# A GNN layer and a pair-routed expert layer on one core: GELU's table load, the first aggregation and the last group's ranks moved

## What is computed

```python
# x: (32, 256, 128), adj: (32, 256, 256)
def _L0_gnn_ref(x, adjacency, epsilon, W1, b1, rms_weight, W2, b2):
    neighbor_sum = jnp.einsum('bnm,bmd->bnd', adjacency, x)
    agg = epsilon * x + neighbor_sum
    h = jnp.einsum('bnd,dh->bnh', agg, W1) + b1            # H = 512
    h = jax.nn.silu(_rmsnorm(h, rms_weight))
    out = jnp.einsum('bnh,hd->bnd', h, W2) + b2
    return out
...
    logits = jnp.einsum('bsd,de->bse', xn, Wr) + br        # E = 8 experts
    top_vals, top_idx = jax.lax.top_k(logits, K)           # K = 2
    w = jax.nn.softmax(top_vals, axis=-1)
...
        h = jax.nn.gelu(jnp.einsum('bsd,dh->bsh', xn, W1[e]) + b1[e], approximate=False)
        y_e = jnp.einsum('bsh,hd->bsd', h, W2[e]) + b2[e]  # H = 256
        y = y + y_e * w_full[..., e, None]
...
    x = x + _L0_gnn_ref(_layernorm(x, axis=-1), adj, ...)
    x = x + _L0_ffn_ref(_layernorm(x, axis=-1), ...)
```

## Time and profile before

| | us |
|---|---|
| median of 3 runs | 423.39 |
| lowest and highest run | 420.89 and 424.64 |
| the profiled execution's own time | 420.72 |
| its span, first to last instruction | 418.9 |

### The profile page before, as it was taken

How to read it: one execution, slowest core, us unless ns; L and a number is a source line. 1 busy time by engine, 2 the same in 40 slices (tenths; PEclk the granted TensorE clock), 3 DMA queues, 4 the chain that set the end, 5 groups by cost and what they waited for, 6 DMA issues and landing times. The chain is left out here.

```text
span 418.9 us, 11379 instructions
## 1 busy us (share of the span) xinstructions
PE 382.8 (91%) x2598; PEld 322.7 (77%) x2598; DVE 301.4 (72%) x1290; ACT 280.2 (67%) x652; POOL 314.2 (75%) x440
## 2 busy tenths in 40 slices
PE   0899999999999999999879899998878999999994
PEld 0457676767777667766659899987768999999994
DVE  5677689898999999988874563665546666756562
ACT  1377677887777887778868556776657787454541
POOL 1223378877787888888888788999857767999984
PEclk9999999999999999999999999999999999999998
DMA  7879974444334442121164324555545543343311
GB/s 236 255 240 323 319 221 138 139 142 139 117 85 132 154 139 79 64 78 53 53 156 126 105 93 137 146 145 154 149 130 140 151 113 104 112 113 106 102 40 38
DMA packets 43473, 57.26 MB, mean 137 GB/s; under 512 B 6224, under 2 KB 36176, under 8 KB 42768
## 3 DMA queue, kind: packets, MB, share of 16 engines
q1 hardware_dynamic: 35200, 36.74, 31.6%
q0 software_dynamic: 6096, 18.52, 12.6%
q10 hardware_dynamic: 2112, 1.27, 1.1%
HBM read 41.80 MB, written 22.31 MB: 153 GB/s over the span
## 5 line engine op out<-in xcount | busy, mean ns | idle before, releaser
L569 POOL DMA_INDIRECT out<-result,rows_in x92 | 90.2, 980 | 29.5 <-DVE result L1553 17.6
L810 PE MATMUL banks<-w_sb,hidden_e 128*128 (+1 forms) x736 | 100.9, 279 | 0.1
L810 PEld LDWEIGHTS banks<-w_sb,hidden_e 128*128 128x128 f32 x736 | 91.0, 192 | 0.7 <-issue 0.3
L950 ACT ACTIVATE hidden_e<-banks 128x512 f32<-128x512 f32 x92 | 55.0, 597 | 44.7 <-PE banks L793 42.9
L512 POOL DMA_INDIRECT rows_dram<-rows_out,row_of x64 | 65.3, 1021 | 14.5 <-issue 10.4
L639 PE MATMUL banks<-gw_sb,agg 128*128 128x512 f32 x128 | 65.2, 595 | 0.9 <-DVE gw_sb L997 0.9
L525 POOL MEMSET space<- 128x620 f32 x100 | 62.9, 629 | 0.1
L661 PE MATMUL banks<-hidden_t,gw_sb 128*128 128x256 f32 x256 | 61.5, 383 | 1.5 <-ACT hidden_t L873 1.5
L661 PEld LDWEIGHTS banks<-hidden_t,gw_sb 128*128 128x128 f32 x256 | 46.5, 190 | 15.3 <-ACT hidden_t L873 7.3
L1090 DVE TENSOR_TENSOR hidden<-banks,rms_bc 128x512 f32<-128x512 f32 x64 | 43.9, 687 | 19.5 <-ACT hidden L858 19.4
L943 ACT ACTIVATE xg_t<-banks,ones 128x128 f32<-128x128 f32 x92 | 33.4, 363 | 24.6 <-PE banks L773 24.5
(11 more groups left out here) (147 smaller groups left out, 738.7 us busy)
## 6 DMA issues: line engine op xcount, KB each, us to landing
rows_in<-rows_dram SPq DMA_DIRECT2D x92, 132.5 KB, 2.2
adj<-adj_t SPq DMA_DIRECT2D x16, 512.0 KB, 4.9
x_tok<-x SPq DMA_DIRECT2D x16, 256.0 KB, 5.3
x_d<-x_t SPq DMA_DIRECT2D x16, 256.0 KB, 4.9
rows_dram<-idle_in POOLq DMA_DIRECT2D x1, 3710.0 KB, 13.8
rows_dram<-idle_in SPq DMA_DIRECT2D x28, 132.5 KB
out<-result,rows_in POOLq DMA_INDIRECT x92, 2.7
w_sb<-w SPq DMA_DIRECT2D x1, 1024.0 KB, 8.2
```

The costliest lines, as they stand in the source:

```text
L569: nc.gpsimd.indirect_dma_start(out=out, out_offset=bass.IndirectOffsetOnAxis(ap=rows_in[:, i % RING][:, IDX_AT:IDX_AT + 1].bitcast(U32), a ...
L810: last = pe.matmul(y_ps(i)[:, w], hidden_e[:, i % 4, w * HCE + c], w2_sb[:, bass.ds(at + c * D, D)], start=(c == 0 and i >= EARLY), stop=( ...
L950: nc.scalar.activation(hidden_e[:, i % 4], h_ps(i), ACT.Gelu).then_inc(gelu_done, 1)
```

## The change

There are three edits.

1. On ACT a one-element GELU activation into a second column of `warm` is put behind the last instruction of the group stage, ahead of the wait for the tile table. The table load goes with it.
2. On PE the ranks of group 15 move from (9, 1) to (10, 1), one tile step later. On DVE `places(z, 0)`, which reads them, moves from (10, 0) to (10, 1), behind the first addition of that step.
3. At the start, DVE's `prep` no longer makes `eps_ident` and the identity part of `turn_by`. This is `prep_ident`, called in step 0 behind the statistics of group 0. `normalise1` of group 0 signals `xn1_half` behind its second tile, and the aggregation of group 0 begins with that and waits for all four tiles only ahead of its second graph.

```diff
+        xn1_half = sem("xn1_half")
...
             def aggregate(g):
-                pe.wait_ge(xn1_ready, g + 1)
+                if g == 0:
+                    pe.wait_ge(xn1_half, 1)
+                else:
+                    pe.wait_ge(xn1_ready, g + 1)
                 pe.wait_ge(adj_ready, g + 1)
...
                 for b in range(2):
+                    if g == 0 and b == 1:
+                        pe.wait_ge(xn1_ready, 1)
...
                 elif at == (4, 1):
                     rank_pairs(NG - 2)
-                elif at == (9, 1):
+                elif at == (10, 1):
                     rank_pairs(NG - 1)
...
+            nc.scalar.activation(warm[:, 1:2], ones[:, 0:1], ACT.Gelu)
             act.wait_ge(table_ready, 2)
...
+            def prep_ident():
                 dve.wait_ge(fixed_in_sbuf, 32)
                 nc.vector.tensor_scalar(eps_ident[:], ident, eps_col[:, 0:1], None, ALU.mult).then_inc(eps_ready, 1)
                 nc.vector.tensor_copy(turn_by[:, 0:D], ident)
...
+                    if g == 0 and t == 1:
+                        last.then_inc(xn1_half, 1)
                 last.then_inc(xn1_ready, 1)
...
                     stats1(g0, 2)
+                if s == 0:
+                    prep_ident()
...
                 elif at == (10, 0):
-                    places(z, 0)
                     share_rows(z, 1)
                 elif at == (10, 1):
+                    places(z, 0)
                     places(z, 1)
                     table(1, 0)
                     find_ends()
```

More of the change, by code:

```diff
@@ L144, in build @@
         eps_col = sb("eps_col", [P, 1])
-        warm = sb("warm", [P, 1])
+        warm = sb("warm", [P, 2])
         gamma_col = sb("gamma_col", [P, 1])
@@ L835, in _ @@
             act.wait_ge(pool_consts, 1)
-            nc.scalar.activation(warm[:], ones[:, 0:1], ACT.Silu)
+            nc.scalar.activation(warm[:, 0:1], ones[:, 0:1], ACT.Silu)
             act.wait_ge(adj_in[0], 16)
```

## The result

The changed kernel's runs had a median of 418.3 us (417.4 to 419.37, 4 runs), and the kernel before 422.7 us (420.89 to 424.64, 4 runs). The ratio is 0.988, with a 95% interval of 0.985 to 0.992: 1.2% faster, between 0.8 and 1.5%. Measured once more in the round of the experiments, the ratio was 0.986 (0.982 to 0.990). The two profiled executions took 420.72 and 417.79 us, 2.9 us apart, with spans of 418.9 and 416.0.

The account below looks back on a forecast made before the run. PE was 91% busy, but SP's alternating loads and fills were taken as the pace from 251.20 us. The start's 1.2 us plus 2.2 for edits 1 and 2, 3.4 off the median 423.4, gave 420.0 us; range 416.8 to 423.2.

Parts of the forecast that it names:

- The point of 1%: Whole kernel: faster by more than 1%, or 4.2 us, got a chance of 0.25; within 1% got 0.72.
- Edit 3, first matmul: Start: PE's first matmul at 8.15 us, 1.36 us earlier, with the normalisation then waiting for the `adj` tile.
- Edit 3, the clock: Start: gain 0.68 us if PE's clock rises when it did before, 1.36 if the rise moves along; 1.2 taken.
- At worst it stays there: Start, DVE: `mix_gw1`, which started at 9.33 us without a wait, would at worst still start then.
- Edit 1: Tile-stage handover: table load covered by a 1.47 us wait, about 0.1 sticking out; PE's wait 1.52 to 0.24; POOL gains 1.12.
- Edit 2: Group 15's ranks: PE's 1.59 us wait goes, POOL gains 1.07 us, `row_of` not later than 239.9 us.
- SP's list as the pace: From 251.20 to about 322 us SP's alternating row loads and fills, 2.51 us a pair, set the time.
- The sum: Whole kernel: SP gains 1.2 + 2.2 = 3.4 us; taken from the median 423.4, this gives 420.0 us.
- The pace of the pairs hides the tile stage: Rival: edits 1 and 2 only lengthen PE's waits for rows, only the start counts: 422.2 us; chance 0.15.
- PE's gain arrives whole: Rival: the pairs' pace gives way too, gain 4.2 to 4.6 us: 419.0 us; chance 0.12.
- The late rank turns against it: Rival: group 15's `row_of`, last scatter and SP's start slip by 2.1 us: 424.3 us, slower; chance 0.10.
- the drain: Rival: about 1.38 us of drain beside ACT's table load takes most of edit 1's gain: 421.1 us; chance 0.05.

Follow-up runs that it names:

- before_again: The kernel before, unchanged, run and traced a second time: 424.04 us, span 422.2 us.
- after_again: The changed kernel, unchanged, measured again beside the single edits: ratio 0.9859 to the kernel before.
- e1_table: The kernel before with only GELU's table load moved to the end of the group stage: ratio 0.9969 to the kernel before.
- e2_ranks: The kernel before with only group 15's ranks one tile step later: ratio 0.9939 to the kernel before.
- e7_pool_longer: The changed kernel with four more 0.63 us memsets on POOL between group 15's second and third scatter: ratio 0.9948 to the kernel before.
- e8_pe_longer: The changed kernel with three more 512-wide matmuls on PE behind tile step 16: ratio 0.9874 to the kernel before.
- e9_warm_fills: The changed kernel with early PE matmuls, 6 fills ahead of SP's wait and 22 behind every second late load: 410.78 us, ratio 0.9639 to the kernel before.
- e5_warm: The changed kernel with 16 small matmuls on PE from about 1 us, ahead of its first wait: ratio 0.9825 to the kernel before.

## Why the prediction was right, and where it was not

The forecast was 420.0 us and 3.4 us of gain; measured were 418.3 us and a gain of 4.4 us between the medians, within the range. Of the 1.7 us by which the time lies below the forecast, 0.7 come from the median of the kernel before, which a fourth run took from 423.4 to 422.7. The forecast sign and the mechanism held: up to SP's start the traces of one round are 3.4 us apart (before_again and after_again), as added up. The point of 1% was passed by a little (1.2%, interval from 0.8), a case that had got 0.25.

- **Edit 3, first matmul.** 8.15 predicted, 8.08 found, and the `adj` tile as what is late next: right (6.71, a wait of 0.76 us for it). The half signal opened no gap.
- **Edit 3, the clock.** The bounds of 0.68 and 1.36 were the right ones. The first trace gave 0.76, near the lower one; six traces with and four without the edit are 1.4 apart on average, at the upper one. I took 1.2. The Trainium skill's page "TensorE: Matmul & The Clock Gate" (section "What's actually happening") says that the monitor's window is free-running and does not start with the kernel. The traces agree in that the first widening came at 14.6 to 15.8 us for the same start. One sign that was named for "wrong" did appear, first matmuls slow for longer than 3.46 us (3.75). It was a bad sign to choose, since the same 3.75 us came in e1_table with the old start. "At worst it stays there", said of `mix_gw1` at 9.33, was wrong: it ran at 10.75, because its bias load took 6.2 us to land in this execution, and 4.7 in the first trace of the kernel before. It was covered by PE's slow sum, and it is one part of what limits the warm start.
- **Edit 1.** The cover held, with 0.4 us to spare instead of the 0.1 us that was to stick out, because the 0.37 us for reading the tile's word no longer stood ahead of the weight copy, which began at 212.51, straight behind the one-element activation. PE's wait went from 1.52 to none, where 0.24 was worked out. The path gained 1.2 us (e1_table), where 1.12 was worked out. No drain stands beside the load: the one-element activation starts at 212.40, 0.02 us behind it. The rule of about 1.38 us more (the Trainium skill, "ScalarE: Activation LUTs", section "What ACT_TABLE_LOAD costs") is not borne out by this trace either.
- **Edit 2.** The wait of 1.59 us went, and the path gained 1.05 us (e2_ranks), where 1.07 was worked out. Both edits together were put at 2.19 us up to POOL's last scatter, and the traces have 2.1 to 2.2. `row_of` was written at 237.1, in time.
- **SP's list as the pace.** Right by three experiments: work on POOL ahead of it costs its full length, work on PE next to nothing, and a shorter list ends sooner. PE's waits for rows were to rise to 8 or 9 us; they stayed at 7.5. That number is one of a single trace: the profile names rows for 7.5 and 3.1 us of waits in the two traces of the kernel before, and for 7.5 and 6.4 in those of the changed one. Further waits at the same place are put down to nothing (6.5 us in before_again, 2.1 in after_again).
- **The sum.** The first pair of traces shows 2.9 us, which is the sum with the low value of the start. What the sum may lack is the granted clock behind the start: executions of the kernel before can fall to 1.2 GHz for some microseconds, and the one profiled before had none of it outside start and end. So the step "taken from the median: 423.4 - 3.4" may leave out a gain of about 1 us by fewer such stretches. That size is an estimate from the runs' clocks, and no experiment showed it by itself. So it is partly luck that 3.4 us came near the measured 4.4: the interval of the first ratio is 3.4 to 6.3 us, and the second measurement gave 6.0 us (4.4 to 7.7), above the forecast gain.

The rivals fell thus. "The pace of the pairs hides the tile stage" fell by the paths of e1_table and e2_ranks and by the ratio of e7_pool_longer. "PE's gain arrives whole" (419.0 us) named a size nearer to the measured one, for a reason that the runs speak against: e7_pool_longer, where only POOL got more work, came out slower, and e8_pe_longer, where PE did, hardly moved. "The late rank turns against it" and "the drain" did not occur.

What stays open: why SP's list took 69 us in two traces and 71 to 73 in the others, how much of the 4.4 to 6.0 us is clock, and why edit 3 alone measured 3.4 us where its first widening shows 1.4.

## What to carry to other kernels

Find the list that paces a stage, and count an edit only by what it does to that list's start and length: 1.59 us taken from the busiest engine was worth 1.05 us, by way of two waits on POOL. Where one queue issues two kinds of transfers in turn, those that nobody waits for soon belong into the queue's idle time and between more of the others: that was worth 1.9 points (e9_warm_fills against e5_warm, measured on two chips), where the three edits together were worth 1.4. And a sum made from one profiled execution needs the clocks of other executions beside it.

## What was not expected of the hardware

- The moment at which PE's clock rises at the start differs between executions of one start: the first widening came at 14.6 to 15.8 us.
- Later stretches of some microseconds at the half clock stand right behind waits of PE as short as 1.5 to 2.5 us, in some executions and not in others. In the changed kernel's trace one stands behind a wait of 2.38 us for rows (granted clock by windows):

```profile
292.00:296.00 4.00, 3.27 (x17) 3.27 (x18) 0.35 (x1) 1.35 (x4) 3.19 (x4) 0.57 0.67 180
```

- The bias load (256 KB) took 4.4 to 6.2 us from its issue to its landing in two executions of one program (after_again and the first trace of the changed kernel), and DVE's mix behind it started at 9.0 and 10.8 us.
- A pair of SP's issues takes 2.5 to 2.7 us, with 0.3 us at most of waits of SP in the whole list, and of this the issue instructions' own times (0.34 and 0.55 us) are a third. Six fills in a row took 8.59 us.
